# Values' fold in half-precision pairs on TensorE, placed after nine tiles of gates

## The reference

```
def ffn(x):                                   # called on layernorm(x), result times 0.5 added to x
    thought = layer_norm(x)[:, -1, :] @ agg_w + agg_b        # last token of each batch only
    for _ in range(4):
        thought = thought + (gelu(layer_norm(thought) @ d1_w + d1_b) @ d2_w + d2_b)
    gate = sigmoid(x @ gate_w + gate_b)
    return layer_norm(x + gate * (thought @ bc_w + bc_b)[:, None, :])

def attn(x):                                  # blocks of 128 tokens, own and previous block
    q, k, v = split(x @ w_attn.T);  q = q / 128
    sim = where(keep, q @ [k_prev, k].T, 0)
    return (relu(sim) ** 2 @ [v_prev, v]) @ w_o.T
```

## Time and profile before

| | us |
|---|---|
| three runs | 2117.34, 2115.19, 2111.64; median 2115.19 |
| profiled execution | 2117.86, its span 2116.6 |
| PE busy | 2037.7 (96% of the span) |
| DVE, ACT, POOL busy | 1173.0, 664.7, 159.0 |
| end of stage 1 / stage 2 in the trace | about 789 / about 1774 |
| fold vo in the trace | about 229 to 371 |

### The profile page before, as it was taken

How to read it: one execution, slowest core, us unless ns; L and a number is a source line. 1 busy time by engine, 2 the same in 40 slices (tenths; PEclk the granted TensorE clock), 3 DMA queues, 4 the chain that set the end, 5 groups by cost and what they waited for, 6 DMA issues and landing times.

```text
span 2116.6 us, 30247 instructions
## 1 busy us (share of the span) xinstructions
PE 2037.7 (96%) x11872; PEld 1037.0 (49%) x11872; DVE 1173.0 (55%) x2108; ACT 664.7 (31%) x931; POOL 159.0 (8%) x281
## 2 busy tenths in 40 slices
PE   8988989999999999998999999999999999999997
PEld 3333433444333446655665555665556564444443
DVE  2321323554344465567676755655555545888887
ACT  0557322433223232222333221211212113444443
POOL 0000000000000010000000000000000000111111
PEclk9999999999999999999999999999999999999999
DMA  8788897988988833348989799898987947555552
GB/s 340 237 311 341 285 353 269 379 319 320 354 338 333 332 132 118 100 140 299 323 294 327 273 320 293 297 347 283 313 290 278 357 149 221 149 151 154 154 149 80
DMA packets 275213, 555.76 MB, mean 263 GB/s; under 512 B 149040, under 2 KB 149248, under 8 KB 274688
## 3 DMA queue, kind: packets, MB, share of 16 engines
q1 hardware_dynamic: 275072, 553.83, 75.5%
HBM read 406.93 MB, written 113.26 MB: 246 GB/s over the span
## 4 chain that ended last, share of the span: by engine, by line
PE 47%; DMA 3%; DVE 2%; SPq 2%; ACT 1%; issue 1%; POOL 0%; ACTq 0%; DVEq 0%
PE product_banks L1023 41%; PE product_banks L1143 3%; PE thought_acc L1208 3%; DMA thought_units<-parts_scratch 1%; DMA gate_arena<-arena 1%; DMA arena<-in_x 0%; SPq L810 0%; DVE thought_units L1754 0%; SPq L944 0%; DMA thought_units<-in_d_w 0%; ACT arena L1315 0%; PE thought_turn L1216 0%; ACT arena L1318 0%; PE thought_acc L1198 0%; DVE arena L1566 0%
## 5 line engine op out<-in xcount | busy, mean ns | idle before, releaser
L1023 PE MATMUL product_banks<-gate_arena,arena 128*128 128x512 f16 x1536 | 354.1, 382 | 0.0
L1023 PE MATMUL product_banks<-wide_a,thought_units 128*128 128x512 f16 x1536 | 331.7, 379 | 0.0
L1023 PE MATMUL product_banks<-gate_arena,wide_a 128*128 128x256 f16 x2688 | 307.5, 274 | 2.4 <-DMA gate_arena<-arena 2.4
L1023 PE MATMUL product_banks<-wide_b,gate_arena 128*128 128x512 f16 x1344 | 301.8, 380 | 0.0
L1023 PEld LDWEIGHTS product_banks<-gate_arena,wide_a 128*128 128x128 f16 x2688 | 260.4, 98 | 59.5 <-issue 28.9
L1054 PE MATMUL product_banks<-wide_a,wide_b 128*128 128x512 f32 x512 | 240.9, 616 | 7.1 <-DMA wide_a<-in_w_attn 6.3
L1023 PEld LDWEIGHTS product_banks<-gate_arena,arena 128*128 128x128 f16 x1536 | 145.0, 98 | 203.6 <-issue 51.0
L1023 PEld LDWEIGHTS product_banks<-wide_a,thought_units 128*128 128x128 f16 x1536 | 150.3, 98 | 181.6 <-DVE arena L1606 0.5
L1023 PEld LDWEIGHTS product_banks<-wide_b,gate_arena 128*128 128x128 f16 x1344 | 127.2, 98 | 167.5 <-issue 24.9
L1423 DVE BATCH_NORM_STATS2 bn_parts<-arena 128x6 f32<-128x512 f32 x256 | 164.3, 684 | 4.4
L1054 PEld LDWEIGHTS product_banks<-wide_a,wide_b 128*128 128x128 f32 x512 | 95.1, 195 | 137.9 <-issue 137.8
(11 more groups left out here) (168 smaller groups left out, 2090.1 us busy)
## 6 DMA issues: line engine op xcount, KB each, us to landing
thought_units<-parts_scratch SPq DMA_DIRECT2D x268, 512.0 KB, 6.1
thought_units<-in_d_w SPq DMA_DIRECT2D x148, 512.0 KB, 6.7
thought_row<-in_d_w SPq DMA_DIRECT2D x76, 512.0 KB, 7.2
arena<-in_x SPq DMA_DIRECT2D x64, 512.0 KB, 8.8
parts_scratch<-thought_units SPq DMA_DIRECT2D x64, 512.0 KB, 6.2
x_scratch<-arena SPq DMA_DIRECT2D x64, 512.0 KB, 6.8
...
```

Of the source, the lines that this page charges most:

```text
L1023: mm = pe.matmul(bank, left(i, k), right(j, k), start=(n == 0), stop=(n == 3 * KD - 1))
```

## The change

- The fold vo is three f16 matmuls for each product, of pairs made from wv ("wv") and the turned w_o ("wo"). New pieces: `top` (DVE reduces a block, 8 for each side), `side_high` (ACT rounds a block) and `side_low` (DVE makes its rest), 8 of each for each side. A pair is written over the block two places before it, so `side_high` e waits for `side_low` e-2. Each step e of the fold's first rows waits for both sides' pairs. The results are scaled back as they leave PSUM.
- The fold vo comes after nine tiles of gates. The turning of w_o is spread over four tiles, the sides' pieces over five.
- `scale_a` is two pieces. `scale_t` is DVE's reduction; in `scale_a` PE multiplies by a constant matrix (one matmul, 128x1), so that the scale comes from the mean over the partitions instead of POOL's maximum, and DVE reads it from a turn bank. There are five scales instead of three.
- `norm_h` is ACT's part of the norm, a piece of its own behind the tile's first gate pieces; `sigmoid` is a piece of its own, one or two gate pieces later.
- `gate_save`, `params` and `half_params` move behind the fold, among the splits of qk and vo, which now run over gates 9 to 27.
- Stage 2's first group begins with the `v` pieces of its first tile, and the wait for the split of vo goes with them.
- `time_of` gives a piece of the fold vo 1.28 instead of 1.83.

```diff
-EARLY, LATE = 3, 4
+EARLY, LATE = 9, 4
...
-        return 1.0 if piece[1:3] == ("qk", 0) else 1.83 * FOLD_SIZES[piece[2]]
+        return 1.0 if piece[1:3] == ("qk", 0) else (1.83 if piece[1] == "qk" else 1.28) * FOLD_SIZES[piece[2]]
...
             out.append(("gate", n, h, third))
-            if n and (h, third) == (1, 0):
-                out.append(("gate_store", n - 1))
+            if n and (h, third) == (0, 0):
+                out.append(("sigmoid", n - 1, 1))
+            if (h, third) == (0, 1) and n + 2 < TILES:
+                out.append(("norm_h", n + 2))
+            if (h, third) == (1, 0):
+                out.append(("sigmoid", n, 0))
+                if n:
+                    out.append(("gate_store", n - 1))
...
+        if n == 0:
+            own = [p for p in products if p[0] == "v" and p[2] == 0]
+            products = own + [p for p in products if p not in own]
...
+def split_side(m):
+    out = [("side_high", m, 0)]
+    for e in range(KD):
+        out += ([("side_high", m, e + 1)] if e + 1 < KD else []) + [("side_low", m, e)]
+    return out
...
-    early = paced([p for n in range(EARLY) for p in plan_gate(n)], wo, 0.9, PE_PIECES)
-    save = [("gate_save", k) for k in range(KD)] + [("params",)] + [("rest",)] * 6 + [("half_params",)]
-    fold_vo = paced(plan_fold("vo"), save, 0.5, PE_PIECES)
+        if n >= 2:
+            wo.append(("top", "wv", n - 2))
+    wo += [("top", "wv", KD - 2), ("top", "wv", KD - 1), ("scale_t", "wv"), ("rest",), ("scale_a", "wv"), ("rest",),
+           ("scale_b", "wv")]
+    wv_splits, wo_splits = (split_side(m) for m in ("wv", "wo"))
+    sides = [("top", "wo", e) for e in range(KD)] + wv_splits[:2] + [("scale_t", "wo")] + wv_splits[2:4]
+    sides += [("scale_a", "wo")] + wv_splits[4:6] + [("scale_b", "wo")] + wv_splits[6:] + wo_splits
+    early = paced([p for n in range(4) for p in plan_gate(n)], wo, 1.45, PE_PIECES)
+    early += paced([p for n in range(4, EARLY) for p in plan_gate(n)], sides, 1.0, PE_PIECES)
...
+    save = [("params",)] + [("rest",)] * 5 + [("half_params",)]
+    for k in range(KD):
+        save += [("gate_save", k)] + [("rest",)] * 3
+    splits = paced(splits, save, 0.75)
...
-                    mm = pe.matmul(bank_ap(key), wide_b[:, e, d * P:(d + 1) * P],
-                                   wide_a[:, e, h * BANK:(h + 1) * BANK], start=(e == 0), stop=(e == KD - 1))
+                        for n, (i, j) in enumerate(((0, 0), (0, 1), (1, 0))):
+                            mm = pe.matmul(bank_ap(key), fold_parts("wv", e)[:, i, d * P:(d + 1) * P],
+                                           fold_parts("wo", e)[:, j, h * BANK:(h + 1) * BANK], start=(e == n == 0),
+                                           stop=(e == KD - 1 and n == PARTS - 1))
...
+            elif kind == "scale_a":
...
+                pe.wait_ge(top_found, SCALE_AT[m] + 1)
+                pe.matmul(turn_ap((kind, m))[:, 0:1], mean_maker[:, :], scale_stat[m][:, KD:KD + 1], start=True,
+                          stop=True).then_inc(turn_full, 1)
...
+            elif kind == "side_high":
...
+                elif e >= 2:
+                    act.wait_ge(side_split[m], e - 1)
+                act.activation(fold_parts(m, e)[:, 0], fold_side[m][:, e, :], ACT.Copy,
+                               scale=scale_stat[m][:, KD + 2:KD + 3]).then_inc(side_high[m], 1)
...
+            elif kind == "side_low":
+                m, e = a
+                dve.wait_ge(side_high[m], e + 1)
...
+                dve.scalar_tensor_tensor(out=fold_parts(m, e)[:, 1], in0=fold_side[m][:, e, :],
+                                         scalar=scale_stat[m][:, KD + 2:KD + 3], in1=fold_parts(m, e)[:, 0],
+                                         op0=ALU.mult, op1=ALU.subtract).then_inc(side_split[m], 1)
```

107 lines of the change are left out of this document (71 added, 36 removed).

## The result

The change takes 2104.29 us (median of 5 runs, 2103.39 to 2107.81), the kernel before 2114.69 beside it (5 runs). The ratio is 0.9952, with an interval of 0.9938 to 0.9967: faster by 10 us. The forecast was 2081, with a range of 2064 to 2101. The sign was right and the size was a third of what I had summed. The span, which is that of one profiled execution, fell from 2116.6 to 2104.3.

The account below looks back on a forecast made before the run. The prediction took TensorE's own work to set the pace, with gains from less work and fewer waits. From 2116.6 us of span its terms summed to 2082.2, given as a time of 2081 us, 8 times in 10 between 2064 and 2101.

Parts of the forecast that it names:

- the fold vo itself: In the fold vo, 384 f16 matmuls replace 256 float32 records and run ends get cheaper: -28.3 us (-26 to -31).
- waits before the fold: Ahead of the fold, TensorE's waits for the norm and w_o's turns, with their slower clock, go: -13.5 us (-8 to -16).
- wait inside the fold: At 293.9 us, TensorE's wait for `t_sums` and its slow clock go as saves move behind the fold: -9.0 us.
- the sides' pieces: In tiles 4 to 8, added reductions and low halves fill VectorE to 67.9 of 68 us: +6 us (0 to +18).
- scale of wv: In tile 3, TensorE's 128x1 matmul newly waits for VectorE's `scale_t`, then runs at slower clock: +9.0 us (+3 to +12).
- opening of stage 2: At stage 2's start, TensorE's wait for the second tile's transposed pair goes, with its clock: -6.6 us (-4 to -7).
- DMA from tile 9 on: After the fold, a shorter stretch with more bytes wants 376 GB/s from DMA: +7 us (0 to +18).
- small ones: Five 128x1 matmuls and their weight loads, 0.1 to 0.3 us each: +1 us.
- the slow rival: In tiles 4 to 8 the sides serialise ScalarE and VectorE: +48 us instead of +6, 2123 us; chance 0.04.
- DMA becomes the bound: In stage 1's second half, DMA at 350 GB/s costs 21 us instead of 7: 2095 us; chance 0.16.
- My own tests: Signs against the forecast: fold triples slower than the gates', waits in tiles 4 to 8 over 15 us, stage 1 ending after 760.
- the fold gains nothing: In the fold, three f16 matmuls cost as much as two float32 records, undoing 28.3 us: 2109 us; chance 0.05.

Follow-up runs that it names:

- The pair of runs without halves: The change with no halves of wv and wo made: fold in float32, ratio 0.9954; fold in half-precision pairs taken from the gate weights, ratio 0.9845; both against the kernel before.

## Why the prediction was wrong, point by point

| term | forecast | measured |
|---|---|---|
| the fold vo itself | -28.3 | 0.216 us a matmul, as forecast; -21 to -23 in place |
| waits before the fold | -13.5 | about -8 |
| wait inside the fold, and the sides' pieces | -9.0 + 6 | +10.3 |
| scale of wv | +9.0 | +9.3 |
| opening of stage 2 | -6.6 | -6.1 (alone 5.1) |
| DMA from tile 9 on | +7 | +6.4 |
| small ones | +1 | not told apart |
| given back in stages 2 and 3, behind the opening | 0 | +2.3 |

With the 28.3 of the fold the measured column comes to -14 (-13 with the small ones), against the 12.3 that the span fell.

The pair of runs without halves splits the miss of 22 us of span in another way. What the change moves besides the fold gains 14.9 us (10 by the ratio) where my terms for it add up to 22.1 (13.5 + 9.0 + 6.6 - 7); pairs gain 21.1 (23) for 28.3; the halves cost 23.7 (22.6) where I had 16 (9 + 6 + 1). By the spans that is some 7 us in each.

**The step that failed is that of the sums**, in two terms. "The wait inside the fold, -9.0" took the wait for the fold's, to be gone with the saves, because the store of a folded row stood in VectorE's way there. That reading of the rows was right, but with the saves gone the store still holds ScalarE for 9.1 of its 11.4 us, and with the fold gone from there the same copy of the sums waits 4.5 and 7.5 us for the kept blocks, without any halves made. "The sides' pieces, +6" was then summed as VectorE's load alone, 67.9 of 68 us. Measured, the two come to 19.3 us: 11.0, 2.2 and 1.6 of waits, 2.7 and 1.7 of clock behind them. Against the 9.0 of before that is +10.3 where I had -3: 13 of the 22 us by which the span missed. The load alone was not the mechanism: VectorE was busy for 84 of 119 us and idle for 8.3 in one piece when it mattered. What I left out was a third queue, that of the fetches. I named ScalarE and VectorE holding each other up, as the slow rival, but priced it as a whole or nothing, and never asked when the kept blocks' two slots are fetched.

**Waits before the fold.** The norm's 5.0 us, w_o's 5.3 and the fold's 0.8 went. Up to the end of tile 2's part (213 in the trace after, 229 before), and without the 5.9 us for the first weights in both, TensorE's waits fall from 19.6 to 11.6 us. What the lower clock cost before, 4.8 us, is matched by some 4.4 at new places: at the start, behind a wait of 2.8 us for a block at 198 and behind one of 2.3 for VectorE's half of a turn at 209, in front of which VectorE had a top of 1.2 us to do. I had put back 2.4 for fetches and nothing for the turns. -8 was my dear end.

**Scale of wv.** The mechanism, the place and the size were right. A part of VectorE's delay was not in my list: it waited 1.6 us for a block of wv.

**DMA.** After the fold TensorE's waits for fetched blocks are 11.7 us against 4.7 from 440 on before, and those for stored parts and their makers fall from 5.6 to 5.0 with the scale's matmul. Between 600 and 700 us DMA stands at

```profile
600.00:700.00 100.00, 93.75 (x565) 36.72 (x563) 37.35 (x82) 29.66 (x39) 4.43 (x12) 1.00 0.97 378
```

so 378 GB/s for 100 us. The bound of 390 was near, and the rival "DMA becomes the bound" did not come: over the whole stretch from 440 to 736 it is 354 GB/s at a share of 0.92. I read that as TensorE arriving later than forecast and so asking for less. The Trainium skill ("DMA: Bandwidth & Descriptors", Specifications) gives about 358 GB/s as the limit of one core at HBM; the trace, with 378 over 100 us, does not agree with it as a ceiling for a core that runs alone.

**The fold.** A run of 12 at 2.76 us holds the forecast of 28.3 as work of TensorE: its product matmuls up to the last turn are busy for 548.2 us, 574.0 before, with stretches at the lower clock in both. That only 21 to 23 us arrive goes with the waits for the thought's blocks and sums, which are 5.8 and 3.0 us longer with the pairs than with float32.

**My own tests.** Waits for VectorE in tiles 4 to 8, with the fold's start, are 14.9 us (11.0, 2.2 and 1.6) without what the clock then costs, just under the 15 that I had named; stage 1 ends at 776, not before 760, and by that test the forecast was wrong. The ends 2057 and 2121 that I gave for all cheap and all dear terms are spans; as times they are 1.4 us less.

**The rivals.** None of the four is what happened: the time lies between "the fold gains nothing" and the forecast, through a part of the slow rival, +13 of its +42 against my term.
